# Two pairs of heads to a period: scores, values of two pairs, scores, then one block on the whole array

## What is computed

```python
q = einsum('bsd,qd->bsq', x, wq)
kv_latent = einsum('bsd,ld->bsl', x, w_kv_down)
k = einsum('bsl,ql->bsq', kv_latent, w_k_up)
v = einsum('bsl,ql->bsq', kv_latent, w_v_up)
q = q * cos + _rotate_half(q) * sin
k = k * cos + _rotate_half(k) * sin
scores = einsum('bhsd,bhtd->bhst', q, k) / sqrt(D) + causal
probs = softmax(scores)
out = einsum('bhst,bhtd->bhsd', probs, v)
s = einsum('bsq,dq->bsd', out, wo)
...
_, topk_idx = top_k(flat_x @ gate_w + gate_b, 2)
e_star = max(topk_idx, axis=-1)
h = gelu(flat_x @ w1[i] + b1[i]); y = h @ w2[i] + b2[i]     # the expert i == e_star
x + s * silu(2 * y)
```

## Time and profile before

| | us |
|---|---|
| median of 3 runs | 305.75 (305.04 to 306.18) |
| the profiled execution | 305.23 |
| its span, first to last instruction | 303.5 |

### The profile page before, as it was taken

The page is one execution under the profiler, slowest core; times in us unless marked ns, Lnnn a source line. Parts: engine busy times, 40 slices in busy tenths (PEclk is TensorE's granted clock), DMA queues, the critical chain, the costliest instruction groups (busy, mean ns, idle before and its releaser), DMA issues.

```text
span 303.5 us, 8596 instructions
## 1 busy us (share of the span) xinstructions
PE 290.1 (96%) x2362; PEld 234.8 (77%) x2362; DVE 227.1 (75%) x905; ACT 243.2 (80%) x871; POOL 217.2 (72%) x321
## 2 busy tenths in 40 slices
PE   8897999999999999999999999999999999899994
PEld 3665888888888888777777789999877777676763
DVE  4889998987786998988888524444398899897651
ACT  4387889898977789989898677777779989799982
POOL 3468878687777779999999963333158999899730
PEclk9999999999999999999999999999999999999999
DMA  6854594979433333333334490000513344344200
GB/s 203 251 132 116 104 297 116 236 172 303 101 68 65 67 77 83 101 88 98 89 88 109 96 288 6 2 2 0 154 38 83 100 120 117 93 115 123 61 19 17
DMA packets 39596, 33.35 MB, mean 110 GB/s; under 512 B 4801, under 2 KB 36674, under 8 KB 39554
## 3 DMA queue, kind: packets, MB, share of 16 engines
q1 hardware_dynamic: 38098, 30.51, 39.1%
q0 software_dynamic: 1024, 2.10, 2.5%
q10 hardware_dynamic: 432, 0.23, 0.3%
HBM read 11.07 MB, written 4.98 MB: 53 GB/s over the span
## 4 chain that ended last, share of the span: by engine, by line
PE 66%; POOL 12%; issue 8%; DVE 6%; DMA 3%; ACT 2%; SPq 2%; POOLq 1%; DVEq 0%; ACTq 0%
PE bank L1128 9%; PE bank L1116 9%; PE bank L1142 8%; PE bank L1339 7%; PE bank L1156 6%; PE bank L1327 6%; POOL probs L477 4%; POOL staged L466 4%; PE bank L1090 4%; PE bank L1144 3%; PE bank L1118 3%; DVE masked L602 2%; PE bank L1106 2%; POOL xn L493 2%; DMA z<-in_woT 2%
## 5 line engine op out<-in xcount | busy, mean ns | idle before, releaser
L906 ACT ACTIVATE pexp<-masked,negmax 128x128 f32<-128x128 f32 (+1 forms) x256 | 114.1, 453 | 2.2 <-DVE negmax L602 2.2
L477 POOL TENSOR_SCALAR probs<-pexp,rden 128x256 f32<-128x256 f32 (+1 forms) x184 | 80.3, 451 | 24.3 <-DVE rden L609 21.7
L602 DVE CUSTOM_DVE_ANT_0 masked<-bank,mask 128x128 f32<-128x128 f32 (+1 forms) x256 | 75.9, 352 | 25.2 <-PE bank L1118 25.0
L466 POOL TENSOR_TENSOR staged<-rot_out 128x512 f32<-128x512 f32 x63 | 80.1, 1273 | 17.5 <-DVE rot_out L593 16.9
L593 DVE TENSOR_TENSOR rot_out<-bank,rot 128x1024 f32<-128x1024 f32 x64 | 77.6, 1214 | 3.9 <-PE bank L1092 2.7
L928 ACT COPY probsT<-bank 128x384 f32<-128x384 f32 x128 | 55.0, 481 | 23.8 <-PE bank L1128 22.8
L1128 PE MATMUL bank<-ident,probs 128*128 128x128 f32 x384 | 54.1, 275 | 1.3 <-POOL probs L477 0.6
L906 ACT ACTIVATION_READ_ACCUMULATOR pexp<-masked,negmax 128x1 f32 x256 | 50.0, 195 | 0.0
L1116 PE MATMUL bank<-qk_sb 64*128 64x256 f32 x256 | 45.0, 427 | 3.2 <-DVE negmax L602 2.5
L1128 PEld LDWEIGHTS bank<-ident,probs 128*128 128x128 f32 x384 | 43.1, 140 | 4.1 <-issue 1.5
L1156 PE MATMUL bank<-vo_sb,ctxT 128*128 128x128 f32 x256 | 39.5, 279 | 0.7 <-ACT ctxT L935 0.7
(11 more groups left out here) (114 smaller groups left out, 485.6 us busy)
## 6 DMA issues: line engine op xcount, KB each, us to landing
qk_sb<-staged SPq DMA_DIRECT2D x128, 128.0 KB, 2.7
w_sb<-in_w SPq DMA_DIRECT2D x2, 1024.0 KB, 6.1
w_sb<-in_w SPq DMA_DIRECT2D x4, 512.0 KB, 4.8
sorted_x<-z SPq DMA_DIRECT2D x1, 1408.0 KB, 8.0
sorted_g<-z SPq DMA_DIRECT2D x1, 1152.0 KB, 5.9
out<-res SPq DMA_DIRECT2D x8, 128.0 KB, 1.9
x_sb<-in_x SPq DMA_DIRECT2D x3, 256.0 KB, 3.3
rot<-in_c_rot SPq DMA_DIRECT2D x1, 512.0 KB, 5.8
```

What stands on the lines that cost most here:

```text
L466: pool.tensor_tensor(staged[:, n % 2, :, m % 2, :], rot_out[:, m % 2, :, 0:S], rot_out[:, m % 2, :, S:2 * S], op=ALU.add).then_inc(staged_ ...
L477: pool.tensor_scalar(probs[:, g % 2, i, c], pexp[:, g % 2, i, c], rden[:, g % 2, i, k:k + 1], 1.0, ALU.mult, ALU.mult).then_inc(probs_read ...
L602: t = dve.tensor_tensor_reduce(masked[:, g % 2, i, c], s_bank[i][:, c], mask[:, c], -1.0, -NEG * 1e8, ALU.add, ALU.min, negmax[:, g % 2, i ...
L906: e = act.activation(pexp[:, g % 2, i, c], masked[:, g % 2, i, c], ACT.Exp, bias=negmax[:, g % 2, i, k:k + 1], scale=-1.0, accum_out=rowsu ...
```

## The change

The slots are taken in twos, as a **period** `s` = 0, 2, ..., 62. TensorE's period is scores of `s + 2`, values of the pairs `s - 2` and `s - 1` together, scores of `s + 3`, then everything that uses the whole array: turn of `s`, projection, two outputs, turn of `s + 1`, projection, and at the end the rows, latents and counting of the early periods. `ALONE` keeps only the last two pairs. `scores` now waits for the row maxima half by half. `TWICE` moves to 22 and 24. `kept_back` gives the last item of a period: its rotation and sum move to the start of the next one, in the periods 24 to 36 and from 42 on. VectorE, ScalarE and GpSimd are put in the order of the period. Which engine does a sum or a scaling hardly changes: `VECTOR_SUMS` is empty. `staged_ready` becomes two semaphores. ScalarE's `normalise` stands first in the periods 2, 6, 10, GpSimd's `rstd` last in the periods 0, 4, 8. `finalise` is split into `gate_sum` and `add_rows`. The scaling of pair 41 moves from the experts' start into period 38.

```diff
-TWICE = (36, 38)
+TWICE = (22, 24)
...
-ALONE = tuple(range(FIRST_DOUBLE)) + (G_LEAD - 2, G_LEAD - 1, B * NP - 2, B * NP - 1)
+ALONE = (B * NP - 2, B * NP - 1)
...
+def items_of(s):
+
+    return [*items(s), *items(s + 1)]
+
+
+def kept_back(s):
+
+    return items_of(s)[-1:] if TWICE[-1] <= s < G_LEAD - 2 or s > G_LEAD else []
...
GpSimd:
+            def period(s):
+                todo, back = items_of(s), kept_back(s)
+                if s:
+                    sums(kept_back(s - 2))
+                if s in (0, 2):
+                    scale(1 + s)
+                if s == 0:
+                    sums(todo[:1])
+                if s + 2 < B * NP:
+                    scale(s + 2)
+                moves(s)
+                if s:
+                    sums(todo[:1] if todo[:1] != back else [])
+                if 0 < s < B * NP - 3:
+                    scale(s + 3)
+                if s == G_LEAD - 2:
+                    first_weights()
+                moves(s + 1)
+                sums(m for m in todo[1:] if m not in back)
+                if s in (0, 4, 8):
+                    rstd(2 + s // 4)
...
VectorE:
+            def ending(s):
+
+                if s == 2:
+                    best(0)
+                    best_at(0)
+                if s in (4, 8):
+                    stats(s // 4 + 2, 2, 4)
+                    variances(s // 4 + 2)
...
+            def period(s):
+                todo, back = items_of(s), kept_back(s)
+                if s + 2 < B * NP:
+                    row_max(s + 2)
...
+                between(s)
+                if s + 3 < B * NP:
+                    row_max(s + 3)
...
+                if s + 2 < B * NP:
+                    denominators(s + 2)
+                    scale(s + 2)
+                for m in todo[:1]:
+                    if m not in back:
+                        rotate(m)
...
+                middle(s)
+                if 0 < s < B * NP - 3:
+                    denominators(s + 3)
+                    scale(s + 3)
+                for m in todo[1:]:
+                    if m not in back:
+                        rotate(m)
+                ending(s)
...
ScalarE:
+            def period(s):
...
+                if s in (2, 6, 10):
+                    normalise(s // 4 + 2)
+                if s in (4, 8, 12):
+                    turned(s // 4 + 1)
...
+                if s + 2 < B * NP:
+                    exponentials(s + 2, 0)
+                    exponentials(s + 2, 1)
+                if s:
+                    ctx_out(s - 2)
+                    turned_probs(s)
...
+                if s + 3 < B * NP:
+                    exponentials(s + 3, 0)
+                    exponentials(s + 3, 1)
+                    scale(s + 2)
+                if s:
+                    turned_probs(s + 1)
+                if 0 < s < B * NP - 3:
+                    scale(s + 3)
...
TensorE:
-                wait(pe, masked_ready, 2 * g)
                 for i, r in enumerate(half_rows):
+                    wait(pe, masked_ready, 2 * g - 1 + i if g else 0)
...
+            def period(s):
+                todo = items_of(s)
+                if s + 2 < B * NP:
+                    scores(s + 2)
...
+                else:
+                    values(s - 2)
+                if s + 3 < B * NP:
+                    scores(s + 3)
...
+                turn(s)
+                if s in (6, 10, 14):
+                    turn_latents(s // 4)
+                for m in todo[:1]:
+                    project(m)
+                output(s - 2)
...
+                output(s - 1)
+                turn(s + 1)
+                for m in todo[1:]:
+                    project(m)
+                if s in (2, 6, 10):
+                    turn_rows(s // 4 + 2)
+                if s in (4, 8, 12):
+                    latents(s // 4 + 1)
+                if s == COUNT_SLOT:
+                    count_tokens()
```

More of the change, by code:

```diff
@@ L287, in build, with program @@
         w_part = [slice(i * S, (i + 1) * S) for i in range(W_PARTS)]
-        def program(start, slot, finish, experts):
+        def program(start, period, finish, experts):
             start()
-            for g in range(B * NP):
-                if g == G_LEAD:
+            for s in range(0, B * NP, 2):
+                if s == G_LEAD:
                     finish(LEAD - 1)
                     experts()
-                slot(g)
+                period(s)
             finish(B - 1)
         def scaler(g, i, k):
-            busy = SCATTER_SLOT <= g - 1 < SCATTER_SLOT + NT or GATHER_SLOT <= g - 1 < GATHER_SLOT + NT
+            busy = indirect(g - 2 - g % 2)
             if g == 0 or g >= B * NP - 3:
@@ L452, in experts @@
                     sp.dma_start(sorted_g.rearrange("(j p) c -> p j c", p=P)[:, n, :], z[:, n, :]).then_inc(g_out, 16)
-            program(start, slot, finish, experts)
+            program(start, period, finish, experts)
             for i in range(2):
@@ L531, in start, with sums, moves @@
                 rotated(AHEAD - 1)
[L533 to L541 removed]
+            def sums(items):
+                for m in items:
+                    if m not in VECTOR_SUMS:
+                        rotated(m)
+            def moves(g):
                 if SCATTER_SLOT <= g < SCATTER_SLOT + NT:
@@ L575, in experts @@
                     step(2 * m + 1, 1)
-            program(start, slot, lambda b: None, experts)
+            program(start, period, lambda b: None, experts)
         @block.vector
@@ L890, in experts @@
                 turned_rows(0, 0)
-                denominators(G_LEAD + 1)
-                scale(G_LEAD + 1)
                 take_y(LEAD - 1)
                 over_tiles(dve, step_of)
-            program(start, slot, finish, experts)
+            program(start, period, finish, experts)
         @block.scalar
@@ L1308, in finish @@
                     turn_tile(0, 0)
+                output(g - 2)
+                if b == B - 1:
+                    values(g - 1)
                 output(g - 1)
```

312 lines of the change are left out of this document (137 added, 175 removed).

## The result

| | before | predicted | after |
|---|---|---|---|
| median, us (4 runs each, in turns) | 305.97 | 310.0 (301 to 312.5) | 339.45 (336.87 to 341.0) |
| ratio to before, 95% interval | | | 1.109 [1.105, 1.113] |
| span of the profiled execution | 303.5 | | 339.1 |

The account below looks back on a forecast made before the run. TensorE was taken as the bound; 8.2 us saved by fewer changes of form, against waits for row maxima and normalise, summed by stage to +5.45, 310.7 us, forecast as 310.0. Range 301 to 312.5 (8 in 10).

Parts of the forecast that it names:

- The forecast's own case: Whole kernel: slower through waits for late row maxima and normalise, 307 to 312 us, chance 0.48.
- S4 to S24: Early stage, between first scores at 28.04 and 107.87 us: 86.9 against 79.83 us, less 1 for overlap, so +6.
- S42 to S62: Late stage, between first scores at 219.69 and 285.85 us: 64.2 against 66.16 us, so -2.0.
- What bounds the kernel now: Whole kernel: TensorE is the bound, though not alone; the clock, granted in full but in the tail, needs no thought.
- The change of form: TensorE's switches between array forms: scores into values 0.11 us, saving 0.22 a late period, 0.38 an early one, 8.2 together.
- VectorE's rooms: Row maxima ahead of second scores, without slack: waits of 7.6 us in periods 2 to 20, 1.2 in 22, 0.65 in 24.
- Normalise behind GpSimd: Periods 2, 6, 10: ScalarE's normalise waits for GpSimd's power and delays TensorE's output by 1.85, 1.5 and 1.5 us, 4.9 in all.
- Late periods: Periods with scatters: 6.78 us instead of 6.71, ScalarE's chain costing half of 0.13; wait for row maxima about nil from 26.
- Experts "unchanged": Expert stage, from the first expert matmul to the scores at 219.69 us: no change in length.
- Tail: End of the kernel: values of pairs 60 and 61 wait for their copy, 18.4 against 17.65 us, +0.75.
- Fast and cancelling cases: Rivals, whole kernel: rooms wide enough, 298 to 304 us, chance 0.27; half of the waits, 304 to 307, chance 0.15.
- GpSimd takes over: Rival, scatter and gather periods: they run at GpSimd's 6.88 us and the expert start slips, 312.5 to 313 us, chance 0.1.

Follow-up runs that it names:

- d1_before_delay: Kernel before, with unread VectorE reductions ahead of the row maxima in slots 28 (five) and 34 (three): 314.35 us, ratio 1.029.
- e2_warm: Changed kernel, with unread TensorE matmuls ahead of the second scores of periods 6, 10 and 22, as long as the waits there: 335.63 us, ratio 1.100.
- e1_accum: Changed kernel, with VectorE's scalings in a form that also adds up what they write (accumulator nobody reads): 330.75 us, ratio 1.086.
- e10_stats_free: Changed kernel, with the accumulator form for the negative means and variances alone, scalings as they were: 336.64 us, ratio 1.103.
- a1_after: The changed kernel itself, measured and profiled again: 339.82 us, ratio 1.109.
- e9_accum_load: e1_accum, with the loads of the sorted rows one period earlier in SP's queue, ahead of the copies of items 44 and 45: 329.35 us, ratio 1.078.
- c2_together: Changed kernel, with accumulator form for scalings and statistics, normalise later, an item kept back from period 20 on, loads first: 318.31 us, ratio 1.041.
- e8_accum_finals: e1_accum, with each finished batch's two VectorE additions moved from a period's end to behind its first row maxima: 334.80 us, ratio 1.091.

## Why the prediction was wrong

The forecast's own case, waits for late row maxima and for normalise, was the right kind of loss. What failed is the price of a wait (its length alone, without the clock) and the durations of VectorE's small instructions (as if GpSimd's work beside them didn't matter). By stage the profile lies above the forecast by 5.4 us (S4 to S24), 9.6 (to the first expert), 3.9 (experts), 9.5 (S42 to S62) and 1.5 (tail).

- **What bounds the kernel now.** "The clock needs no further thought, since it was granted in full" was the first failed step. It was granted in full in a kernel whose TensorE hardly waited; I forecast a dozen waits and priced each at its length. In the periods 6 and 10 the waits of 1.3 us were followed by the clock's fall or not, and the fall cost 2.6 us more each time. The wait of 3.5 us of d1_before_delay cost 5.8; but behind the one of 3.2 us in period 22 a held clock gave only 0.6 us back (e2_warm), since VectorE was late anyway.
- **The change of form: right.** Values start 0.85 us after the first scores (139.92 and 140.77), as the walk had it with 0.11 for scores into values, and a late period is 6.71 us where nothing else disturbs (e1_accum).
- **VectorE's rooms: the mechanism right, a term missing, the sum lucky.** The walk gave 85.8 us for S4 to S24; with the clock held (e1_accum) it is 87.0. That near agreement is luck in part. The waits for the row maxima cost more than the 7.6 us forecast. Where nothing is late, the turn starts 3.15 us into a period (period 20); over the periods 2 to 20 of e1_accum it starts 10.5 us later than that in all, since behind each late start the second half of the scores comes later still (the turn is 1.31 us behind the second scores instead of 0.86). Normalise cost 1.6 instead of 4.9. The prediction's 74.4 us of work with these two are 86.5. Single terms were off both ways: 0.5 and 0.65 us forecast for the periods 6 and 10 and 1.3 each measured, 1.3 for period 4 and 0.5 measured; and for period 22 1.2 where 3.2 was. What is missing in 6 and 10, and part of what is missing in 22, is an instruction held up by GpSimd (1.32 us; 1.32 and 1.25). All durations of "ending" were read from the kernel before, where they fell beside other work of GpSimd: I took durations as belonging to instructions, where they depended on what GpSimd did beside them. Two rows of the kernel before would have told:

```profile
137.68 0.73 DVE L620 TENSOR_SCALAR probs<-pexp,rden 128x128 f32<-128x128 f32 x1
...
141.74 0.29 DVE L620 TENSOR_SCALAR probs<-pexp,rden 128x128 f32<-128x128 f32 x1
```

- **Normalise behind GpSimd: size right, sum wrong.** 4.9 us forecast; uncovered (e10_stats_free) it is 1.88 + 1.44 + 1.54 = 4.86. But I added it to the waits for the row maxima and took 1 us off. In fact the two overlap in the same periods, by 3.3 us of 4.9 (e1_accum: 1.07 + 0.21 + 0.30).
- **Late periods: wrong in the changed kernel.** 6.78 forecast, 7.34 to 7.96 measured. I asked whether ScalarE's or GpSimd's chain would exceed TensorE's, and not whether VectorE, with zero slack (2.35 against 2.29, by the prediction's own numbers), had anything just ahead of its row maxima. "From 26 on the rotation is kept back and the wait is about nil" is the failed sentence; the scaling stands there, 1.6 us instead of 0.29. With it in the accumulator form the periods are 6.81 us on average.
- **Experts "unchanged": wrong.** I followed TensorE's and GpSimd's queues across the move of the items, not SP's. They took 3.9 us more in this profile and 2.8 in a1_after's. With the load one period sooner the stretch from S40 to S42 is at the kernel before's length again (55.7 us in e9_accum_load, 55.9 before), so the load's place in SP's queue accounts for the loss there.
- **S42 to S62: wrong sign.** -2.0 forecast, +7.6 measured. 2.1 of it went with c2_together; 2.3 had gone with the scaling's form alone (e1_accum). Of the rest, in e1_accum, 1.2 to 1.4 us in each of the periods 50, 52 and 54, which finish a batch, is VectorE's two additions ahead of the row maxima (e8_accum_finals at 50 and 52); I had allowed 0.6 in all. Period 42 (7.9 instead of 6.8) and the last two of the stage (7.3 and 7.2 instead of 6.2) weren't tried; their cause stays open.
- **Tail:** +0.75 forecast, +2.3 measured; no run tried it, and the cause stays open. TensorE's waits there for ScalarE's copies are 0.90, 1.52, 0.47 and 0.47 us.
- **Rivals and range.** Fast and cancelling cases had 0.42 of the chance, on VectorE's average room. "GpSimd takes over" named the right engine by the wrong way: it isn't full (64% busy), it holds VectorE up. The range's upper end took in each wait once; no case was there for a wait that costs more than itself.

## What to carry over

Where a change takes slack out of an order, list what stands directly ahead of each newly critical instruction and ask of every duration whether it is the instruction's own. Here it was VectorE's small instructions between SBUF and SBUF, beside GpSimd's work, that stretched, and one line with two durations in one trace was the sign. Price a forecast wait of TensorE with and without a fall of the clock behind it, and don't add waits of one period on two engines: take the later one, and expect the other to appear when the first is mended. Walk all queues over a moved step, the DMA queue too.

## What was not expected of the hardware

- VectorE's instruction of 4 elements a row took 1.32 us beside a sum of GpSimd and 0.15 us in the accumulator form. A scaling of 128 columns took 0.29 us or up to 2.06; one of 1.93 stood through a scatter and the sum behind it without a turn in between.
- The accumulator form costs 0.35 instead of 0.29 us and 0.08 for reading the accumulator, and in none of the 41 scalings of e1_accum was it held up.
- A wait of TensorE of 1.3 us was followed by 1.2 GHz 5 times in 14 (8 in 18 with the longest executions), within one execution too (periods of 13.01 and 10.47 us in a1_after); one of 3.5 us cost 5.8. Work that nobody reads, as long as the wait, kept 2.4 GHz.
